# Four sums of a Mamba-style layer's preparation: GpSimd additions against accumulating transfers, with a new placement of the preparation's steps

## The reference, cut to what matters

```
xn = layernorm(x) * g + b;   xp = xn @ proj + pb;   z = silu(xp)
for direction d in (forward, backward):          # backward: tokens reversed
    xs    = softplus(xp @ conv_d + cb_d)          # 256 channels
    dbc   = xs @ dbc_w                            # 32 rank, 16 B rows, 16 C rows
    delta = softplus(dbc[:32] @ dtp_w + dtp_b)    # 256 channels
    u     = delta * xs
    h_n[t] = exp(-A_n * delta[t]) * h_n[t-1] + u[t] * B_n[t]      # n = 0..15
    y_d   = sum_n h_n * C_n + xs * D
x = x + z * (y_fwd + y_bwd)
```

## Time and profile before

| | before |
|---|---|
| median of 3 runs | 21142.09 us |
| the profiled execution, its time | 21148.16 us |
| its span | 21146.5 us |
| VectorE busy | 20040.8 us, 95% |
| GpSimd busy | 19961.2 us, 94% |
| TensorE matmul busy | 18486.7 us, 87% |
| ScalarE busy | 11624.6 us, 55% |
| mean share of the 16 DMA engines | 53.7% by queue (50.2 + 2.6 + 0.7 + 0.1 + 0.1) |

### The profile page before, as it was taken

One profiled execution on the slowest core, in us unless ns is written; L12 is line 12 of the kernel. 1 busy time (PEld: TensorE's weight loads), 2 busy tenths in 40 slices (PEclk: granted clock), 3 DMA queues, 4 the chain that ended last, 5 costly groups with the idle time before them and its releaser, 6 DMA issues.

```text
span 21146.5 us, 192534 instructions
## 1 busy us (share of the span) xinstructions
PE 18486.7 (87%) x46368; PEld 7537.6 (36%) x46368; DVE 20040.8 (95%) x11904; ACT 11624.6 (55%) x12409; POOL 19961.2 (94%) x8174
## 2 busy tenths in 40 slices
PE   7888888888888888888888888888888888888888
PEld 3333333333333333333333333333333333333333
DVE  7999999999999999999999999999999999999999
ACT  5555555555555555555555555555555555555554
POOL 7999999999999999999999999999999999999998
PEclk9999999999999999999999999999999999999999
DMA  4555555555555555555555555555555555555555
GB/s 160 183 186 183 186 185 183 187 183 190 180 186 185 185 185 181 189 183 181 189 181 185 184 184 185 185 187 180 187 185 184 184 184 187 182 185 185 186 185 176
DMA packets 1101818, 3886.20 MB, mean 184 GB/s; under 512 B 147584, under 2 KB 158336, under 8 KB 1100416
## 3 DMA queue, kind: packets, MB, share of 16 engines
q1 hardware_dynamic: 1023616, 3733.38, 50.2%
q0 software_dynamic: 26112, 100.67, 2.6%
q10 hardware_dynamic: 50688, 36.88, 0.7%
HBM read 3744.62 MB, written 134.22 MB: 183 GB/s over the span
## 4 chain that ended last, share of the span: by engine, by line
issue 35%; POOL 20%; DVE 19%; PE 17%; DMA 4%; ACT 4%; DVEq 1%; ACTq 1%; POOLq 0%; SPq 0%
DVE ring L807 12%; POOL ring L352 11%; PE y L666 10%; DVE bv L791 5%; DMA c<-c_rows 4%; PE bv L656 3%; POOL delta L392 3%; PE bank L684 3%; ACT dA L500 2%; POOL parts L382 1%; POOL v L360 1%; DVE w L821 1%; POOL u L400 1%; PE bank L731 1%; POOL dbc L377 1%
## 5 line engine op out<-in xcount | busy, mean ns | idle before, releaser
L352 POOL TENSOR_TENSOR ring<-ring,c 128x1024 f32<-128x1024 f32 x6144 | 14326.7, 2372 | 218.9 <-DVE ring L807 214.5
L666 PE MATMUL y<-ring,ident 128*128 128x512 f32 x24576 | 11788.8, 607 | 621.3 <-POOL ring L352 527.8
L807 DVE TENSOR_TENSOR_SCAN ring<-dA,bv 128x1024 f32<-128x1024 f32 x5376 | 12024.4, 2272 | 100.3
L500 ACT ACTIVATE dA<-delta,a_step 128x1024 f32<-128x1024 f32 x5376 | 6022.4, 1146 | 2835.7 <-DVE ring L807 2241.8
L791 DVE TENSOR_TENSOR bv<-u,bv 128x1024 f32<-128x1024 f32 x5376 | 6333.3, 1214 | 842.5 <-POOL u L400 396.1
L666 PEld LDWEIGHTS y<-ring,ident 128*128 128x128 f32 x24576 | 4756.5, 195 | 4961.0 <-issue 3524.0
L656 PE MATMUL bv<-parts,select 128*128 128x512 bf16 x10752 | 3303.5, 389 | 1853.9 <-DVE ring L807 1836.9
L656 PEld LDWEIGHTS bv<-parts,select 128*128 128x128 bf16 x10752 | 729.9, 99 | 5758.4 <-DVE ring L807 5152.3
L500 ACT ACTIVATE bv<-delta,a_step 128x1024 f32<-128x1024 f32 x768 | 859.5, 1119 | 2441.7 <-DVE ring L807 2325.2
L360 POOL TENSOR_TENSOR v<-u,v 128x1024 f32<-128x1024 f32 x768 | 1812.3, 2360 | 128.8 <-DMA v<-c_rows 127.7
L807 DVE TENSOR_TENSOR_SCAN ring<-bv,v 128x1024 f32<-128x1024 f32 x768 | 1739.3, 2265 | 31.0 <-ACT bv L500 31.0
(11 more groups left out here) (65 smaller groups left out, 10688.8 us busy)
## 6 DMA issues: line engine op xcount, KB each, us to landing
c<-c_rows SPq DMA_DIRECT2D x6144, 512.0 KB, 4.4
v<-c_rows SPq DMA_DIRECT2D x768, 512.0 KB, 4.9
out_dram<-z POOLq DMA_DIRECT2D x96, 1024.0 KB, 11.9
pre<-out_dram SPq DMA_DIRECT2D x88, 1024.0 KB, 5.2
c_rows<-dbc ACTq DMA_DIRECT2D x192, 128.0 KB, 1.9
pre<-in_x_dram SPq DMA_DIRECT2D x8, 1024.0 KB, 5.1
out_dram<-in_x_dram SPq DMA_DIRECT2D x8, 1024.0 KB, 18.2
raw_w<-in_L_conv_proj_w_dram ACTq DMA_DIRECT2D x12, 256.0 KB, 5.6
```

The lines of the kernel that those rows point to most:

```text
L352: nc.gpsimd.tensor_tensor(ring[k % NR][:], ring[k % NR][:], c_sb[k % NC][:], ALU.mult).then_inc(p_ready, 1)
L500: nc.scalar.activation(to[:], delta_of(d, s)[:, c, :], ACT.Exp, scale=a_step[s][:, c, n:n + 1]).then_inc(da_ready, 1)
L666: mm = pe.matmul(y[:, half(h)], ident[:], ring[k % NR][:, half(h)], start=(k % HALF_TILES == 0), stop=(k % HALF_TILES == HALF_TILES - 1), ...
L807: nc.vector.tensor_tensor_scan(h, a, b, 0.0, ALU.mult, ALU.add).then_inc(h_ready, 1)
```

## The change

The four additions on GpSimd become transfers from SBUF to SBUF with `accum_op=ADD`, issued by GpSimd: 1 MB each, on a semaphore of their own that counts 16 for each transfer. What GpSimd waited for ahead of an addition, it now waits for ahead of the product of that slot (`before_sums`). u waits for both transfers of its direction. Who waited for `xs_ready` or `delta_ready` waits for the transfers' counts. In the first preparation, which has no products, a memset of one column of a small tile stands ahead of each transfer. The constants of the preparation, two of the `SHARED` tiles (35 to 33, 45 to 41) and the distances `B_AHEAD` and `V_AHEAD` are new. `HELD` is new too; with LAG = 5 the condition that it is in never holds either way, so that `add_up(k - 5)` is due in slot k before and after.

```diff
-    SHARED = (9, 19, 23, 29, 35, 45, 55, 59)
-    B_AHEAD, V_AHEAD = 5, 6
-    LAG, HELD = 5, 2
+    SHARED = (9, 19, 23, 29, 33, 41, 55, 59)
+    B_AHEAD, V_AHEAD = 2, 5
+    LAG, HELD = 5, -1
...
-    MEAN_AT, CENTRE_AT, SQUARE_AT = (3, 4), (8, 10), (7, 10)
-    VAR_AT, RSTD_AT, NORM_AT = (9, 11), (11, 15), (9, 16)
-    PROJ_AT, XP_AT = (15, 15, 19, 19), (16, 16, 19, 19)
-    CONV_AT = ((22, 23, 25, 27), (29, 31, 33, 35))
-    CONV_OUT_AT = ((21, 23, 28, 29), (29, 30, 33, 34))
-    XS_LOG_AT, XS_AT = ((31, 32), (35, 35)), (35, 39)
-    DBC_AT, DBC_OUT_AT = ((37, 39), (47, 49)), ((37, 39), (47, 48))
-    DTP_AT, DTP_OUT_AT = ((41, 41, 41, 42), (49, 51, 51, 51)), ((40, 41, 42, 42), (50, 50, 52, 52))
-    HI_AT, REST_AT, MID_AT, PARTS_AT = (40, 49), (44, 53), (45, 57), (47, 55)
-    DELTA_LOG_AT, DELTA_AT, U_AT = ((43, 47), (55, 55)), (47, 55), (47, 57)
-    DIAG_AT, A_STEP_AT = 49, 53
-    GATE_AT = 37
-    LOADX_AT = 50
+    MEAN_AT, CENTRE_AT, SQUARE_AT = (1, 3), (4, 5), (2, 3)
+    VAR_AT, RSTD_AT, NORM_AT = (6, 10), (10, 10), (8, 10)
+    PROJ_AT, XP_AT = (11, 16, 19, 19), (13, 16, 18, 18)
+    CONV_AT = ((22, 23, 25, 27), (30, 31, 33, 35))
+    CONV_OUT_AT = ((21, 23, 24, 29), (31, 32, 32, 35))
+    XS_LOG_AT, XS_AT = ((29, 29), (38, 39)), (28, 41)
+    DBC_AT, DBC_OUT_AT = ((37, 39), (45, 48)), ((37, 38), (49, 49))
+    DTP_AT, DTP_OUT_AT = ((41, 42, 42, 43), (50, 51, 51, 52)), ((40, 41, 41, 45), (50, 50, 50, 51))
+    HI_AT, REST_AT, MID_AT, PARTS_AT = (40, 49), (42, 52), (44, 57), (45, 55)
+    DELTA_LOG_AT, DELTA_AT, U_AT = ((45, 48), (53, 54)), (47, 54), (51, 58)
+    DIAG_AT, A_STEP_AT = 40, 53
+    GATE_AT = 36
+    LOADX_AT = 53
...
-    SKIPS = ((13, 9), (51, 55))
+    SKIPS = ((15, 9), (47, 49))
...
                     if k == XS_AT[j]:
-                        pool.wait_ge(ln_done, n * CHAINS + (conv_chain[j] + 1))
-                        pool.wait_ge(conv_out, n * (2 * FILLS) + (j + 1) * FILLS)
-                        nc.gpsimd.tensor_tensor(xs_of(d, s)[:], xs_of(d, s)[:], scratch[j][:],
-                                                ALU.add).then_inc(xs_ready, 1)
+                        pool.dma_start(xs_of(d, s)[:], scratch[j][:], accum_op=ALU.add).then_inc(xs_ready[j], 16)
                     if k == DELTA_AT[j]:
...
+                        pool.dma_start(delta_of(d, s)[:], scratch[j][:], accum_op=ALU.add).then_inc(delta_ready[j], 16)
                     if k == U_AT[j]:
-                        pool.wait_ge(delta_ready, n * 2 + (j + 1))
+                        pool.wait_ge(xs_ready[j], n * 16 + 16)
+                        pool.wait_ge(delta_ready[j], n * 16 + 16)
...
+            def before_sums(k, n):
+                for j in range(DIRS):
+                    if k == XS_AT[j]:
+                        pool.wait_ge(ln_done, n * CHAINS + (conv_chain[j] + 1))
+                        pool.wait_ge(conv_out, n * (2 * FILLS) + (j + 1) * FILLS)
+                    if k == DELTA_AT[j]:
+                        pool.wait_ge(ln_done, n * CHAINS + (delta_chain[j] + 1))
+                        pool.wait_ge(dtp_out, n * (2 * FILLS) + (j + 1) * FILLS)
...
+                    if more:
+                        before_sums(k, it + 1)
                     product(it, k, s)
```

More of the change, by code:

```diff
@@ L141, in conv_seq_kernel @@
         eps = sb("eps", [P, 1])
+        mark = sb("mark", [P, 5])
         c_rows = nc.dram_tensor("c_rows", (2, DIRS, BC, T), F32, kind="Internal").ap()
@@ L175, in conv_seq_kernel @@
         gate_ready = sem("gate_ready")
-        xs_ready = sem("xs_ready")
+        xs_ready = [sem(f"xs_ready{j}") for j in range(DIRS)]
         dbc_ready = sem("dbc_ready")
@@ L184, in conv_seq_kernel @@
         parts_ready = sem("parts_ready")
-        delta_ready = sem("delta_ready")
+        delta_ready = [sem(f"delta_ready{j}") for j in range(DIRS)]
         u_ready = sem("u_ready")
@@ L292, in load_x @@
                 if not early(n, 1):
-                    sp.wait_ge(delta_ready, (n - 1) * 2 + 1)
+                    sp.wait_ge(delta_ready[0], n * 16)
                 sp.dma_start(pre[:], src[b]).then_inc(x_loaded, 16)
@@ L401, in prepare, with first_prepare @@
                                                 ALU.mult).then_inc(u_ready, 1)
+            def before_sums(k, n):
[6 more added lines that the diff above has]
+                        pool.wait_ge(dtp_out, n * (2 * FILLS) + (j + 1) * FILLS)
+            def first_prepare(k, n, s):
+                if k in XS_AT or k in DELTA_AT:
+                    before_sums(k, n)
+                    q = (*XS_AT, *DELTA_AT).index(k)
+                    nc.gpsimd.memset(mark[:, q:q + 1], 0.0)
+                prepare(k, n, s)
             def finish(it, s, b):
@@ L421, in tail @@
                 pool.wait_ge(gated, it * DT + DT)
-                nc.gpsimd.memset(v_sb[:, 0:1], 0.0)
+                nc.gpsimd.memset(mark[:, 4:5], 0.0)
                 finish(it, s, b)
-            run_layers(nothing, slots, prepare, nothing, tail, nothing, pool)
+            run_layers(nothing, slots, first_prepare, nothing, tail, nothing, pool)
         @block.scalar
@@ L491, in tile_exp @@
                     act.wait_ge(a_ready, it + 1)
-                    act.wait_ge(delta_ready, it * 2 + 2)
+                    for j in range(DIRS):
+                        act.wait_ge(delta_ready[j], it * 16 + 16)
                 if k in SHARED:
@@ L555, in prepare @@
                             act.wait_ge(dtp_ready, n * (2 * FILLS) + (j * FILLS + i + 1))
-                            act.wait_ge(xs_ready, n * 2 + (j + 1))
+                            act.wait_ge(xs_ready[j], n * 16 + 16)
                             if d == 0 and not early(n, 1):
@@ L596, in rstd @@
                 act.wait_ge(var_ready, n * 2 + (h + 1))
-                act.wait_ge(delta_ready, n * 2)
+                for j in range(DIRS):
+                    act.wait_ge(delta_ready[j], n * 16)
                 th = tmp[:, 0, half(h)]
@@ L674, in add_skip @@
                     pe.wait_ge(diag_ready, it * DT + DT)
-                    pe.wait_ge(xs_ready, it * 2 + 2)
+                    for j in range(DIRS):
+                        pe.wait_ge(xs_ready[j], it * 16 + 16)
                 for h in range(NH):
@@ L719, in prepare @@
                         if k == DBC_AT[j][h]:
-                            pe.wait_ge(xs_ready, n * 2 + (j + 1))
+                            pe.wait_ge(xs_ready[j], n * 16 + 16)
                             if j:
```

## The result

The changed kernel takes 21784.54 us (median of 4 runs, 21755.04 to 21799.62) against 21140.12 for the kernel before on the same chip: ratio 1.0307, 95% interval 1.0294 to 1.0319. The forecast was 21,145 with a range from 20,840 to 21,400. The profiled execution's span is 21768.2 us, 621.7 more than before. By the starts of the first scans of the passes, a pass takes 225.32 us in the mean where it took 218.77: +6.55, or 622 over 95 passes. So all of it lies in the steady passes: the first scan starts 3.9 us later than before, and what follows the start of the last pass is 4.3 us shorter.

The account below looks back on a forecast made before the run. VectorE was taken as the bound. On the profiled 21148 us, 95 x (-3.36 - 0.4 + 3.4 + 0.3) = -6 and +11 once gave 21153; the runs' median, 6 lower, gave 21147, forecast as 21,145, range 20,840 to 21,400.

Parts of the forecast that it names:

- What bounds the kernel: VectorE is the bound, its own pace untouched; at most its idle 3.36 + 3.62 us a pass can be won.
- What leaves GpSimd, and the wait for u: GpSimd is relieved of 14.8 us a pass; VectorE's 3.36 us wait for u goes, with 1.1 to spare.
- The landing: Transfers land after 11.9 us, bounded by 8.3 and 13.5; hidden, the two tight ones 0.2 us from the edge.
- the first rival: Landing above 12.1 us makes TensorE's slot 45 and u late: 1.4 to 2.9 us a pass, 21,340 named; chance 0.27.
- The new places on TensorE: Preparation matmuls in even slots delay `rep_b`, slot 51's 1.61 wait goes: +3.4 us a pass in sum.
- slots 6, 16 and 52: nothing: TensorE steps in these slots, three ahead of a shared tile, cost VectorE nothing.
- The rest, "I take 0.3 a pass": SP loads v two steps ahead, giving GpSimd 4.6 us for a landing of 4.9: 0.3 us a pass.
- above, 3 us: Upper end for v loads: 3 us if tile 55's load, beside delta's transfer, takes twice as long and slack is used.
- if VectorE waits for v: A sign named in advance that the forecast is wrong: VectorE waiting for v in the changed trace.
- ScalarE, "0, and up to 1": ScalarE's blocks end 0.2 us or more ahead of the scan needing the next decay: cost 0, up to 1.
- two nearly equal terms: In the sum per pass: -3.36 - 0.4 us for VectorE's waits around u, +3.4 for TensorE's new places.

Follow-up runs that it names:

- experiment 3: Changed kernel with B_AHEAD 4 in place of 2 and each transfer issued right behind its product, ahead of that slot's u * B: 21,387 us (1.0122).
- Experiment 4: TensorE's steps moved out of slots 10, 30, 42, 48 and 50: on the changed kernel 21,465 us, on that of experiment 3 (skips 55, 57) 21,209.
- Experiment 1: Each part alone on the kernel before: transfers with old places 21,937 us; new places, shared tiles and distances with sums on GpSimd 22,140 us.

## Why the prediction was wrong, by its steps

- **What bounds the kernel**: right. VectorE's instructions take what they took; the time is in its waits.
- **What leaves GpSimd, and the wait for u**: right but for 0.3 us. From its start to the next instruction an issue takes 0.61 us in the median, 0.78 expected, and GpSimd's busy time fell by 14.1 us a pass, 14.8 expected. u was to be ready 1.1 us early and is late by 0.26 a pass in the mean; in experiment 3, where the row of tile 55 is in time, it isn't late.
- **The landing**: right, and on the safe side. Line 386's transfers land in 7.0 to 11.3 us, line 388's in 7.8 to 12.0, bounded as 8.3 to 13.5; no landing passed the 12.1 from which the first rival would decide, and TensorE hardly waited for xs. By this trace the estimate of 4.4 us for 1 MB from the fit in the Trainium skill (DMA: Bandwidth & Descriptors, Anatomy of one DMA) is too short for an accumulating transfer into SBUF among other traffic; the fastest took 7.0.
- **The new places on TensorE**: the mechanism is right and so are the listed sizes. Expected 1.2, 1.1, 1.2, 1.2 and 0.3 us a pass at tiles 13, 35, 45, 51 and 53; measured 1.43, 0.98, 1.26, 1.26 and 0.41, and the 1.6 at tile 54 went. Experiment 4 removes the first four but for some us. What failed here is "slots 6, 16 and 52: nothing", at slot 6: 1.14 a pass came at tile 10 or 11, which I put down to its variance and to the halved clock after VectorE's block of z and two centred halves; I had reckoned TensorE at its full clock and without a backlog. The 0.3 at tile 17 isn't slot 16's, since `rep_b(17)` is issued ahead of it: it comes in 24 passes. In one of them (6728 to 6732 us) it stands behind an `add_up` of 3.3 us at a granted clock of 0.57, after TensorE had been idle for 2.1 us.
- **The rest, "I take 0.3 a pass"** for v rows: this is the term that failed most, eight times too small. The row of tile 55 took 9.7 us and not 4.9, in the queue that I had found to have 1.6 us of slack; I had named the collision ("above, 3 us") and taken the near end. It measured 2.47 before scan 59, and "if VectorE waits for v" was one of my own signs of being wrong.
- **Tile 62 or 63, not in the sum**: 1.44 a pass, where there had been 0.27. 0.85 of it lies outside the seventh passes, where TensorE's clock falls behind the wait for v; 0.59 is the late weight matrix. Experiment 3 takes away the wait for v and all but 0.08 of the 0.85, and leaves 0.56 of the 0.59: of 398 us it won, these are 235 and 77.
- **ScalarE, "0, and up to 1"**: 0.75 more a pass at scan 9. It falls in ten passes of 7 to 10 us each, the first of a layer, where ScalarE issues the fourteen loads of the next layer's weights between the squares and the decay of tile 9: in one pass from 7373.6 to 7388.1 us. Experiment 1 tells whose cost it is: the new places with additions have 73 us there, the transfers in the old places 5. I tie it to the squares, which now stand ahead of these loads, but no run moved them alone.
- **A cost with no step**: VectorE's 5376 multiplications take 6392.5 us and not 6333.3. Two that follow each other overlap by 0.1 us, and a wait between them takes that away: 0.6 a pass, an estimate of the cause by the 542 more waits for `rep_b`.

Together, against +6.55 measured: 2.2 (v) + 1.2 (tile 62) + 1.1 (tile 11) + 0.3 (tile 17) + 0.7 (scan 9) + 0.6 (overlap) + 0.3 (listed slots) + 0.3 (u) = 6.7, on a forecast of -0.06; of the small ones left out, the largest is 0.4 less at tile 6. The sign of my sum rested on two nearly equal terms; nearly every term left out was on the slow side. I take that to be because a new placement has its slack unmeasured where the old one's waits stand in the trace.

## What to carry to other kernels

Moving work from a full engine to a transfer frees its queue but turns 4.5 us of work into 8 to 12 of latency; price first where the result is waited for, then what the moves that cover it cost elsewhere (here each part alone was 3.8 and 4.7% slower, and only the old places with a dozen constants adapted to the landing made a gain of 2%). When a chain is found with a slack of 1 to 2 us, take every load in it at its slowest row beside the new traffic, not at its median. Look through the passes that differ too, such as the one that loads the next layer's weights: a few long waits there can weigh as much as a short one in every pass. A wait in a chain of engines can be paid again where TensorE's clock falls behind it.

## What the runs showed of the hardware that I had not expected

The v rows' median hardly moved with the new traffic (4.9 to 5.3 us over 768 loads), though the row that goes out 3.6 us behind a 1 MB accumulating transfer took 9.7 in the median (5.0 before), and a weight matrix of 256 KB asked for 0.6 us behind one took 9.0 (3.0 before). The next image's load went from 5.2 to 7.2. An accumulating transfer from SBUF to SBUF is not much faster than one to DRAM: medians of 8 to 11.5 us against 11.8 in the same kernel.
